# A deformable convolution block: the first sampling table written once and gathered as two lines, and x loaded in channel halves

## What is computed

```python
h = bn_lrelu(dcnv2(x, w_off1, b_off1, w1, b1, k=1, pad=0))   # 512 -> 256 channels, 1 tap
h = bn_lrelu(dcnv2(h, w_off2, b_off2, w2, b2, k=3, pad=1))   # 256 -> 512 channels, 9 taps
return x + h

def dcnv2(x, w_off, b_off, w, b, k, pad):
    om = conv(x, w_off) + b_off               # offsets oy, ox and a mask for each tap
    val = bilinear(x, oy + base_y, ox + base_x) * sigmoid(mask)
    return einsum("ncphw,ocp->nohw", val, w) + b
```

## Time and profile before

| | us |
|---|---|
| median of 3 runs (3485.56 to 3488.94) | 3487.9 |
| the profiled execution: its time | 3491.2 |
| its span | 3489.4 |
| stage 1: start to the first gather (L574) | 0 to 318.3 |
| stage 2: first gather (L574) to first gather of stage 3 (L911) | 318.3 to 847.3 |
| stage 3 | 847.3 to 3489.4 |

### The profile page before, as it was taken

The page is one execution under the profiler, slowest core; times in us unless marked ns, Lnnn a source line. Parts: engine busy times, 40 slices in busy tenths (PEclk is TensorE's granted clock), DMA queues, the critical chain, the costliest instruction groups (busy, mean ns, idle before and its releaser), DMA issues.

```text
span 3489.4 us, 56281 instructions
## 1 busy us (share of the span) xinstructions
PE 3173.4 (91%) x16416; PEld 2588.7 (74%) x16416; DVE 2905.5 (83%) x6326; ACT 1551.4 (44%) x3347; POOL 2419.4 (69%) x1701
## 2 busy tenths in 40 slices
PE   6996777774999999999999999999999999999999
PEld 5995444442887878888888788888878888887888
DVE  6545788875888889898898889889888998988986
ACT  3563222222444444444444444444444444445443
POOL 0002666663878878788888888778788888888882
PEclk9998888886999999999999999999999999999999
DMA  9996887875999999998999999999899999999994
GB/s 297 315 341 226 291 292 258 292 285 204 361 368 327 353 339 324 362 348 318 354 349 335 321 364 343 330 339 357 321 345 356 341 324 345 354 328 349 349 345 146
DMA packets 454395, 1125.07 MB, mean 322 GB/s; under 512 B 42796, under 2 KB 198956, under 8 KB 454112
## 3 DMA queue, kind: packets, MB, share of 16 engines
q0 software_dynamic: 244672, 891.09, 69.7%
q1 hardware_dynamic: 121376, 143.90, 12.2%
q10 hardware_dynamic: 88192, 88.61, 7.5%
HBM read 986.42 MB, written 137.04 MB: 322 GB/s over the span
## 4 chain that ended last, share of the span: by engine, by line
PE 65%; issue 4%; DVE 3%; ACT 2%; ACTq 0%; DMA 0%; DVEq 0%; POOL 0%; POOLq 0%
PE psum_acc L1043 56%; PE psum_val L1029 10%; DVE val L977 2%; ACT val_too L929 1%; ACT val L926 1%; ACT z_sb L947 1%; DVE val_lo L984 1%; DMA gather<-table,plan_in 0%; ACTq L946 0%; POOL gather L911 0%; DVE val_too L977 0%; ACTq L944 0%; ACT val_hi L938 0%; DVEq L973 0%; DMA plan_in<-plan 0%
## 5 line engine op out<-in xcount | busy, mean ns | idle before, releaser
L911 POOL DMA_INDIRECT gather<-table,plan_in x1521 | 2095.0, 1377 | 538.6 <-issue 349.1
L977 DVE SCALAR_TENSOR_TENSOR val<-gather,plan_in,val 128x256 f32<-128x256 f32 x3807 | 1581.8, 477 | 123.3 <-ACT val L926 106.9
L1043 PE MATMUL psum_acc<-val_hi,w_hi 128*128 128x512 f32 (+1 forms) x3096 | 1232.2, 398 | 58.2 <-ACT z_sb L947 58.2
L1043 PE MATMUL psum_acc<-val_hi,w_lo 128*128 128x512 f32 (+1 forms) x3096 | 1205.0, 389 | 0.0
L1043 PE MATMUL psum_acc<-val_lo,w_hi 128*128 128x512 f32 (+1 forms) x3096 | 1200.5, 388 | 0.0
L938 ACT ACTIVATE val_hi<-psum_val 128x1024 fp32r<-128x1024 f32 (+1 forms) x387 | 391.7, 1012 | 1369.3 <-PE psum_acc L1043 1369.3
L1043 PEld LDWEIGHTS psum_acc<-val_hi,w_hi 128*128 128x128 f32 x3096 | 583.0, 188 | 174.8 <-ACT z_sb L947 65.2
L926 ACT ACTIVATE val<-gather,plan_in 128x256 f32<-128x256 f32 x1521 | 694.4, 499 | 25.4 <-DMA gather<-table,plan_in 25.3
L1043 PEld LDWEIGHTS psum_acc<-val_hi,w_lo 128*128 128x128 f32 x3096 | 582.1, 188 | 120.6
L1043 PEld LDWEIGHTS psum_acc<-val_lo,w_hi 128*128 128x128 f32 x3096 | 583.5, 188 | 108.1
L984 DVE TENSOR_TENSOR val_lo<-psum_val,val_hi 128x1024 fp32r<-128x1024 f32 (+1 forms) x387 | 464.9, 1201 | 185.8 <-ACT val_hi L938 184.8
(11 more groups left out here) (75 smaller groups left out, 2151.1 us busy)
## 6 DMA issues: line engine op xcount, KB each, us to landing
stage<-x SPq DMA_DIRECT2D x70, 512.0 KB, 6.6
out<-stage SPq DMA_DIRECT2D x140, 256.0 KB, 5.1
area_a<-x SPq DMA_DIRECT2D x68, 384.0 KB, 6.5
gather<-table,plan_in POOLq DMA_INDIRECT x1521, 6.5
table<-y_stage ACTq DMA_DIRECT2D x26, 896.0 KB, 6.8
table<-area_a ACTq DMA_DIRECT2D x26, 896.0 KB, 5.7
table<-y_stage ACTq DMA_DIRECT2D x26, 768.0 KB, 6.4
table<-area_a ACTq DMA_DIRECT2D x26, 768.0 KB, 12.3
```

Of the source, the lines that this page charges most:

```text
L911: nc.gpsimd.indirect_dma_start(gather2[:, slot(r, i), :, :].rearrange("p q c -> p (q c)"), None, table2, bass.IndirectOffsetOnAxis(ap=row. ...
L977: nc.vector.scalar_tensor_tensor(out=v, in0=gather2[:, slot(r, i), q, :], scalar=weight(r, i, q), in1=v, op0=ALU.mult, op1=ALU.add).then_i ...
L1043: last = nc.tensor.matmul(psum_acc[:, oc, 0:n], a[:, w, oc * P:(oc + 1) * P], b[:, r % 2, kt, 0:n], start=(w == 0 and a is w2_hi and b is ...
```

## The change

`table1` has one pixel per row (256 floats, 1 KB), and `table_writes` writes each half chunk of y once, at one place instead of two. The two writes of zero edges of `table1` go, too. The gather of a tile becomes two indirect DMAs on POOL, one for each image line of the sample, each fetching 2 KB per pixel (two neighbouring rows of 1 KB). For that `index1` has two row numbers per pixel, and `plan` has one more DVE instruction, which subtracts 52 from the lower line's. The corners lie in another order in the slot, so DVE picks its weight by `CORNERS`. DVE waits for 32 instead of 16 counts on a slot's semaphore.

The loads of x of a quarter that lies within one image are cut by channels instead of pixels: each DMA brings two of the four channel blocks in runs of 384 pixels (1536 bytes). The number of DMAs and their bytes stay.

```diff
-    table1 = nc.dram_tensor("table1", [TABLE_ROWS, 2 * C_MID], f32, kind="Internal").ap()
+    table1 = nc.dram_tensor("table1", [PIXELS, C_MID], f32, kind="Internal").ap()
...
-    cut = end - first if first < end < first + count else count // 2
-    return [((first + o) // IMAGE, (first + o) % IMAGE, o, n) for o, n in ((0, cut), (cut, count - cut))]
+    k = C_OUT // P
+    if first < end < first + count:
+        n = end - first
+        return [(first // IMAGE, first % IMAGE, 0, n, 0, k), (first // IMAGE + 1, 0, n, count - n, 0, k)]
+    return [(first // IMAGE, first % IMAGE, 0, count, k0, k0 + k // 2) for k0 in (0, k // 2)]
...
-            for row, col in ((WIDTH, 0), (0, C_MID)):
+            for row, col in places:
...
-                            table_writes(act, table1, y_stage, c, half, table_written[half])
+                            table_writes(act, table1, ((0, 0),), y_stage, c, half, table_written[half])
...
-                                index1[:, tile0:tile0 + n].unsqueeze(2), nth + 1)
+                                index1[:, 1, tile0:tile0 + n].unsqueeze(2), nth + 1)
+                    link_in_plan(nc.vector.tensor_scalar(index1[:, 0, tile0:tile0 + n], index1[:, 1, tile0:tile0 + n],
+                                                         float(-WIDTH), None, ALU.add))
...
                     if t >= SLOTS:
                         pool.wait_ge(sampled, t + 1 - SLOTS)
                     pool.sem_inc(gather_cleared, 1)
-                    nc.gpsimd.indirect_dma_start(
-                        gather1[:, t % SLOTS, :, :].rearrange("p q c -> p (q c)"), None,
-                        table1, bass.IndirectOffsetOnAxis(ap=index1[:, t:t + 1], axis=0))\
-                        .then_inc(gathered[t % SLOTS], 16)
+                    for line in range(2):
+                        nc.gpsimd.indirect_dma_start(
+                            gather1[:, t % SLOTS, 2 * line:2 * line + 2, :].rearrange("p q c -> p (q c)"), None,
+                            table1, bass.IndirectOffsetOnAxis(ap=index1[:, line, t:t + 1], axis=0))\
+                            .then_inc(gathered[t % SLOTS], 16)
...
-                                dve.wait_ge(gathered[t % SLOTS], (t // SLOTS + 1) * 16)
+                                dve.wait_ge(gathered[t % SLOTS], (t // SLOTS + 1) * 32)
```

More of the change, by code:

```diff
@@ L39 @@
 SLOTS = 8
+CORNERS = (0, 2, 1, 3)
 def pixel_constants():
@@ L51, in pixel_constants, with blocks_of_x @@
     return where.transpose(1, 0, 2).copy(), shift
-def pieces(first, count):
+def blocks_of_x(first, count):
     end = (first // IMAGE + 1) * IMAGE
-    cut = end - first if first < end < first + count else count // 2
-    return [((first + o) // IMAGE, (first + o) % IMAGE, o, n) for o, n in ((0, cut), (cut, count - cut))]
+    k = C_OUT // P
[3 more added lines that the diff above has]
+    return [(first // IMAGE, first % IMAGE, 0, count, k0, k0 + k // 2) for k0 in (0, k // 2)]
 def deformable_kernel(nc, x, w1, norm1, w_off2, w2, norm2, norm2_col, b_off1, b_off2, where, shift,
@@ L136, in deformable_kernel @@
         weights1 = part(4 * TILES).rearrange("p (q t) -> p q t", q=4)
-        index1 = part(TILES).bitcast(u32)
+        index1 = part(2 * TILES).bitcast(u32).rearrange("p (v t) -> p v t", v=2)
         bias1 = part(C_MID)
@@ L288, in _ @@
                             sp.wait_ge(x_split, CHUNK * (c - 1) + j + n)
-                        for image, px, o, count in pieces(c * CHUNK_PX + j * P, n * P):
-                            sp.dma_start(x_sb[:, :, j * P + o:j * P + o + count],
-                                         x[image].rearrange("(k p) n -> p k n", p=P)[:, :, px:px + count])\
+                        for image, px, o, count, k0, k1 in blocks_of_x(c * CHUNK_PX + j * P, n * P):
+                            sp.dma_start(x_sb[:, k0:k1, j * P + o:j * P + o + count],
+                                         x[image].rearrange("(k p) n -> p k n", p=P)[:, k0:k1, px:px + count])\
                                 .then_inc(x_loaded[quarter], 16)
@@ L313, in _ @@
                 pool.wait_ge(edge_cleared, 1)
[L314 to L317, removed]
+                for row, col in ((0, 0), (PIXELS, C_MID)):
+                    pool.dma_start(table2[row:row + WIDTH, col:col + C_MID], offsets1_flat[0:WIDTH, 0:C_MID])\
+                        .then_inc(edge_written, 16)
                 pool.wait_ge(w1_scaled, 1)
@@ L361, in copy_y @@
                         if j == j0:
-                            act.wait_ge(table_written[half], (c + 1) * 32)
+                            act.wait_ge(table_written[half], (c + 1) * 16)
                     act.wait_ge(x_used, c * CHUNK + j + 1 + MOST_BACK)
@@ L394, in _ @@
                 for half in range(2):
-                    act.sem_inc(table_written[half], 32)
-                act.wait_ge(edge_written, 64)
+                    act.sem_inc(table_written[half], 16)
+                act.wait_ge(edge_written, 32)
                 chunk(0, first=True)
@@ L404, in _ @@
                 for half in range(2):
-                    act.wait_ge(table_written[half], (CHUNKS + 1) * 32)
+                    act.wait_ge(table_written[half], (CHUNKS + 1) * 16)
             @block.vector
@@ L686, in _ @@
                                 act.wait_ge(h_ready, c * CHUNK + j0 + n)
-                                table_writes(act, table2, h_stage, c, half, table_written[half])
+                                table_writes(act, table2, ((WIDTH, 0), (0, C_MID)), h_stage, c, half, table_written[half])
                         if b == 1 and c:
```

10 lines of the change are left out of this document (5 added, 5 removed).

## The result

| | before | changed |
|---|---|---|
| median, us | 3488.0 | 3536.0 |
| range, us | 3485.6 to 3488.9 | 3526.4 to 3561.8 |
| ratio | | 1.0135, 95% interval 1.0096 to 1.0173 |
| profiled span | 3489.4 | 3540.9 |
| first gather of stage 2 | 318.3 | 297.9 |

The change makes the kernel 1.35% slower. The forecast was 3648, with a range from 3555 to 3692: right in direction, wrong in size. The spans differ by 51.5 us, and the stages say how that is made up: stage 1 is 20.4 us shorter (forecast 6), the gathers of stage 2 take 550.7 instead of 481.7 us, 69.0 more (forecast 165.7), the tail behind them is 4.0 shorter, and stage 3 is 6.8 longer.

The account below looks back on a forecast made before the run. Stage 2 was taken as bound by DVE before and by POOL after: gathers 422.5 + 212.4 + 12.5 = 647.4 us against 481.7, +165.7; with stage 1 at -6 and stage 3 at 0, 3648 us, range 3555 to 3692.

Parts of the forecast that it names:

- POOL becomes the bound of stage 2: Stage 2: POOL limits a chunk at 50.2 us, its wait for DVE gone; gathers take 165.7 us more.
- The price of a gather: Stage 2: a 2 KB gather costs POOL 0.94 us as before, pitch 1.25 us; 338 take 422.5 us.
- Rival C: Stage 2: a gather of 2 KB costs POOL half, pitch 0.77 us; total 3482 to 3495 us; chance 0.04.
- A fed block of three: Stage 2: three tiles with all gathers landed, 5.75 us of unbroken DVE work passing one gather; costs POOL 4.5 us.
- The starved block: Stage 2: a block whose last gather is late; its run from corner 1 on blocks POOL, 4.0 us for three tiles.
- A fed block of two: Stage 2: two tiles with all gathers landed cost POOL 2.6 us blocked, two such blocks per chunk.
- The all-starved bound: Stage 2, low end: all blocks starved at the low price, 14.0 us blocked per chunk, gathers +119 us.
- Rival A: Stage 2: POOL is no longer held through a run, gathers pass at the next operation; 3453 us; chance 0.06.
- E: Stage 2: more than thought passes between the operations of a starved block; 3500 to 3580 us; chance 0.07.
- Rival B: Stage 2: the block lasts one DVE operation and the table2 wait stays; only stage 1 counts, 3482 us; chance 0.03.
- Stage 1, -6 us: Stage 1: PE sets the pace; shorter w2 wait 3, start and clock 1, end 2 us; between 0 and -14.
- The wait for `table2`: Stage 2: DVE's 56.4 us wait may disappear or not, without effect, since POOL issues freely in it.

Follow-up runs that it names:

- e1: The kernel before with each gather of the first sampling cut into two of 2 KB, nothing else changed; 3591.7 us, ratio 1.0205 to the kernel before.
- e14: The changed kernel with DVE's blocks of stage 2 set to 4, 2, 4 and 3 tiles; ratio 1.0137 to the kernel before.
- e10: The kernel before with two buffers for h in stage 2, so DVE waits only for table2 writes two chunks back; ratio 0.9988.
- e11: The kernel before with SyncE issuing the second write of table1 and two buffers for h; ratio 0.9985.
- e16: The kernel before with SyncE issuing the second write of table1 and two buffers for h, run again; 3478.2 us, ratio 0.9966.
- e2: The kernel before with the loads of x by channels alone; ratio 1.0011 to the kernel before.
- e3: The changed kernel with the old loads of x (runs of 768 bytes); ratio 1.0118 to the kernel before.
- e5: The changed kernel with DVE's blocks of stage 2 cut to one tile each; 3478.5 us, ratio 0.9952 to the kernel before.
- e6: The changed kernel with DVE's sums of corners 0 to 2 in PSUM and two PSUM banks for the transposes of h; ratio 0.9989 to the kernel before.
- e8: The changed kernel with one tiny DVE memset ahead of corner 2 and corner 3 of each block; ratio 0.9964 to the kernel before.

## Why the prediction was wrong

- **POOL becomes the bound of stage 2.** Right. POOL's wait for DVE fell from 115 to 7 us, and e1 shows it without the rest.
- **The price of a gather.** Right: 0.95 us for 2 KB as for 4 KB, pitch 1.25 us; 338 x 1.25 = 422.5 us. Rival C fell.
- **A fed block of three.** Right: its gather lasts 5.45 us, 4.5 of them held. The forecast had 13 such blocks, the trace has 16, of 4.0 us on average.
- **The starved block, 4.0 us (3.4 to 4.6).** This is the step that failed. It measured 1.2 us on average over 23 blocks. The prediction bounded it by fed blocks and by one gather in the middle of a run, and took "the run from corner 1 on" for closed as a whole. In fact the first six operations behind a pause let a gather through at the next operation, and only gathers asked for later can be held to the seam. The blocks of three that starved held 28.2 us where the forecast had 104: 76 of the 98 us between 225 and 127.
- **A fed block of two, 2.6 us.** Too dear as well: 1.4 us on average over 21, of which only seven held more than 2.3 us. The prediction took the price from the one chunk that it read. All blocks of two held 31.3 us where the forecast had 62.4, 31 us; three more fed blocks of three and 3.7 us outside the blocks take 10 of that back.
- **The all-starved bound of 119 us.** It was made from the same mispriced run, so the range had no end where the result lay. Rival A, in which a gather passes at the next operation, was too far the other way, and E (3500 to 3580, chance 0.07) was the case that came.
- **Rival B, one instruction's wait, the rule of the Trainium skill ("SBUF — State Buffer", section "Who interferes with whom").** The traces agree with it early in a run (at most 1.28 us in the first six operations) and not late: e14's 7.37 us.
- **Stage 1, -6 us.** Wrong, -20.4. The row of 38.98 busy us was read as "what PE can do"; 331 matmuls fit into the same 40 us. The prediction had asked for the bytes of the second write and not for its issue: 1.00 us of ACTq for two against 0.38 for one, with the rounding of x behind it. In the steady chunks that is 8.8 us of the 20.4; 10.0 lie in the first four chunks, and their cause is open. The end of the stage gained 2.3 us (DVE goes on 5.0 us behind the last issue instead of 7.3), as forecast 2; the wait for w2 fell from 6.1 to 5.0 us, forecast 3.
- **The wait for `table2` doesn't matter.** Right for the changed kernel. For the kernel before it was part of the bound, but e10, e11 and e16 show that only 6 to 10 us were to be had from it (474, 471 and 471 us of gathers against 481), since the wait for gathers takes its place.
- **Loads of x by channels, 0.** Right as far as e2 and e3 can tell, within the 5 us by which the first gather varies.

## What to carry to other kernels

Count the instructions that a DMA costs its issuing engine before its bytes: here one issue fewer on ScalarE took 1.1 us off each chunk of 20.1 in a stage whose DMA engines were full, and one gather more per tile on GpSimd cost 69 us beside long runs of VectorE and nothing beside short ones (e5). Where GpSimd gathers beside VectorE operations with two SBUF inputs, look at how long VectorE's unbroken runs are: cut them with a pause or with a tiny operation without inputs (0.06 us twice a block took the held time from 109 to 136 us down to 51). And price a wait from rows in the same position (here: how many operations behind the last pause), not from the longest ones.

## What the runs showed of the hardware

- A gather of GpSimd was held by unbroken VectorE operations with two SBUF inputs up to the seam between two blocks: at most 1.21, 3.54, 5.45 and 7.37 us with blocks of one to four tiles. Asked for in the first six operations of a run it took at most 1.28 us (675 gathers in seven traces); from the seventh on it could be held. Why a run closes only then stays open.
- With one input of three in five of VectorE's operations in PSUM the longest gather was 1.80 us, with both inputs of all in SBUF 5.45; of those asked for 16 operations into a run, ten of ten took 0.95 us in e6, nine of ten 5.45 in the changed kernel.
- An operation of VectorE that reads nothing (a memset of one column, 0.06 us) shortens the hold: the longest gather went from 5.45 to 2.25 us in e8.
- With 128 row numbers an indirect DMA takes GpSimd 0.95 us for 2 KB each and 0.94 for 4 KB each.
- Two DMA issues in a row kept ScalarE's queue for 1.00 us, one for 0.38 us, and the instruction behind them waited.
- The kernel before took 3488.0, 3492.7, 3502.1, 3520.6 and 3942.3 us in five sets of runs. The slowest set lost it mostly in stage 3: between 2000 and 2400 us 290 GB/s moved and the granted clock was 0.91 in e10, against 342 GB/s and 1.00 in the kernel before of the first set. The sets of 3520.6 and 3942.3 us ran on a chip of the same number, 12, so it isn't shown that the chip makes the difference.
